# One decoder layer on one core: x1 kept in one layout, two normalisations moved from VectorE to ScalarE, other instruction orders

## The reference, cut to what matters

```
# 1. linear attention, 128 wide: q, k, v from x;
#    sq = elu(q)+1, sk = elu(k)+1
a  = (g*memory(sq, M, z) + (1-g)*causal(sq, sk, v)) @ w_o.T
x1 = layernorm(x + a)
# 2. convolution along the 512 columns; 8 positions make a head (32 heads)
kv[i,j] = ctx[i] * ctx[j]                 # i, j: positions of one head
y[i,j]  = conv(kv[i,j], kernel[head]) + D[head] * kv[i,j]
c[j]    = sum over i of y[i,j] * q[i]     # q is x1
x2 = layernorm(x1 + c)
# 3. gated feed-forward, 1408 wide, weights unpacked from 4 bits
h  = silu(x2 @ w_gate.T) * (x2 @ w_up.T)
x3 = layernorm(x2 + rmsnorm(h @ w_down.T))
```

## Time and profile before

| | |
|---|---|
| median of three runs | 532.0 us |
| the profiled execution | 532.28 us, its span 530.6 us |
| granted TensorE clock, mean | 0.988 |
| PE busy | 504.4 us (95%) |
| ACT busy | 400.5 us (75%) |
| POOL busy | 383.6 us (72%) |
| DVE busy | 370.9 us (70%) |
| DMA queue q1 | 98746 packets, 40.14 MB, 31.1% |
| packets under 512 B | 72570 |

### The profile page before, as it was taken

The page is one execution under the profiler, slowest core; times in us unless marked ns, Lnnn a source line. Parts: engine busy times, 40 slices in busy tenths (PEclk is TensorE's granted clock), DMA queues, the critical chain, the costliest instruction groups (busy, mean ns, idle before and its releaser), DMA issues.

```text
span 530.6 us, 11816 instructions
## 1 busy us (share of the span) xinstructions
PE 504.4 (95%) x3612; PEld 372.5 (70%) x3612; DVE 370.9 (70%) x1161; ACT 400.5 (75%) x962; POOL 383.6 (72%) x449
## 2 busy tenths in 40 slices
PE   8998986999999999999999999999999999999992
PEld 6776775668876677667766776777677667776651
DVE  2876665898887677867777787778686876674223
ACT  4478864046999988878877887888689868978981
POOL 2576883696899499959976996799679968972231
PEclk9999998999999999999999999999999999999997
DMA  8443766325026666313213320322041102001001
GB/s 230 138 100 82 167 142 134 79 56 140 12 61 132 156 111 150 71 48 115 56 24 86 86 62 4 114 64 59 0 119 40 40 1 80 2 2 40 1 21 40
DMA packets 98786, 40.63 MB, mean 77 GB/s; under 512 B 72570, under 2 KB 90106, under 8 KB 98746
## 3 DMA queue, kind: packets, MB, share of 16 engines
q1 hardware_dynamic: 98746, 40.14, 31.1%
HBM read 27.46 MB, written 12.66 MB: 76 GB/s over the span
## 4 chain that ended last, share of the span: by engine, by line
PE 67%; POOL 7%; issue 7%; SPq 6%; ACT 5%; DVE 3%; DMA 3%; POOLq 0%; DVEq 0%; ACTq 0%
PE p_cv L129 6%; PE p_cv L131 6%; PE p_cv L130 6%; PE p_n L1284 5%; PE p_n L1283 5%; PE p_n L1282 5%; SPq L401 5%; PE p_qk L1269 4%; PE p_x L1269 4%; PE p_x L1271 4%; PE p_qk L1271 4%; PE p_qk L882 3%; PE p_s L1269 3%; PE p_s L1271 3%; POOL shared L283 2%
## 5 line engine op out<-in xcount | busy, mean ns | idle before, releaser
L1120 ACT ACTIVATE p_qk<-p_qk,rescale 128x256 f32<-128x256 f32 x192 | 79.8, 464 | 24.6 <-PE p_qk L1271 24.2
L129 PE MATMUL p_cv<-kv_hi,toe 128*128 128x288 f16 x320 | 92.6, 289 | 5.9 <-DMA toe<-toeplitz_rows 4.5
L1088 POOL TENSOR_TENSOR h_lo<-w,h_hi 128x256 f16<-128x256 f32 x88 | 68.9, 795 | 35.6 <-ACT h_hi L1137 35.5
L130 PE MATMUL p_cv<-kv_lo,toe 128*128 128x288 f16 x320 | 92.5, 289 | 0.0
L131 PE MATMUL p_cv<-kv_hi,toe 128*128 128x288 f16 x320 | 92.5, 289 | 0.0
L283 POOL TENSOR_TENSOR shared<-shared 128x1024 f32<-128x1024 f32 x32 | 75.6, 2362 | 11.5 <-DVE shared L243 11.4
L1120 ACT ACTIVATE p_x<-p_x,rescale 128x256 f32<-128x256 f32 x192 | 79.8, 468 | 0.8
L1282 PE MATMUL p_n<-wd_hi,h_hi 128*128 128x512 f16 x176 | 66.7, 379 | 0.0
L1283 PE MATMUL p_n<-wd_lo,h_hi 128*128 128x512 f16 x176 | 66.7, 379 | 0.0
L1284 PE MATMUL p_n<-wd_hi,h_lo 128*128 128x512 f16 x176 | 66.7, 379 | 0.0
L1269 PE MATMUL p_qk<-x_hi,wg_hi 128*128 128x256 f16 x256 | 63.0, 273 | 2.4 <-DVE w L1183 1.5
(11 more groups left out here) (167 smaller groups left out, 1237.3 us busy)
## 6 DMA issues: line engine op xcount, KB each, us to landing
toe<-toeplitz_rows SPq DMA_DIRECT2D x16, 512.0 KB, 3.7
cnat<-in_ctx SPq DMA_DIRECT2D x128, 32.0 KB, 2.0
xq<-x_blocks SPq DMA_DIRECT2D x16, 256.0 KB, 5.6
xr<-x_rows SPq DMA_DIRECT2D x16, 256.0 KB
out_x<-fin SPq DMA_DIRECT2D x16, 256.0 KB
ring<-in_x SPq DMA_DIRECT2D x6, 512.0 KB, 4.1
...
```

The lines of the kernel that those rows point to most:

```text
L129: nc.tensor.matmul(dst, hi, kh, start=(mb == 0), stop=False)
L130: nc.tensor.matmul(dst, hi, kl, start=False, stop=False)
L1088: nc.gpsimd.tensor_tensor(h_lo[:, i, :], h32[:, i % 2, :], h_hi[:, i, :], ALU.subtract).then_inc(h_low, 1)
L1120: done = nc.scalar.activation(sums, sums, ACT.Copy, scale=rescale[:, p - 1, part * GI + i:part * GI + i + 1])
```

## The change

Parts of the change:

- `x1_blocks` is gone. A slot is stored by one DMA; its eight block stores go. q is loaded from `x1_rows` by `load_q`, 16 DMAs of 32 x 8 x 32 elements (32 KB) per group, where there were 2 of 256 KB. A semaphore `in_xq` counts to 128 per half.
- `xq` and `qv` are single tiles now. `turn_q` of a half waits for all 16 terms of the group before (8 before), and the first term of a group waits for both halves.
- x2's normalisation moves: VectorE forms `nm2 = -mean * rs` (128 x 1), ScalarE applies `x * rs + nm2` (`nx`). The same for x3: `e` is now VectorE's small `shift`, `z` is ScalarE's `finish`.
- In the first stage `means` and `variances` work on a slot's two columns one at a time (128 x 1 twice, not 128 x 2).
- All lists of order are new.

```
-        self.xq = [sb(f"xq{p}", [P, D], F32) for p in range(2)]
+        self.xq = sb("xq", [P, B, KD, 32], F32)
-        self.qv = [sb(f"qv{p}", [P, 2 * LB * 64], F32) for p in range(2)]
+        self.qv = sb("qv", [P, HG * 256], F32)
...
+    def norm_x2(g, t):
+        act.wait_ge(cv.nm2_made, g * 2 + t + 1)
+        nc.scalar.activation(cv.x2n[:, t, :], cv.x2n[:, t, :], ACT.Identity, scale=cv.rs2[:, t],
+                             bias=cv.nm2[:, t]).then_inc(cv.x2_made, 1)
...
     def turn_q(g, p):
-        dve.wait_ge(cv.in_xq[p], (g + 1) * 16)
-        wait(dve, cv.termed, (g - 1) * 16 + 8 * p + 8)
+        dve.wait_ge(cv.in_xq[p], (g + 1) * 128)
+        wait(dve, cv.termed, g * 16)
...
         if lb == 0:
-            dve.wait_ge(cv.q_kept, g * 2 + h // 2 + 1)
+            dve.wait_ge(cv.q_kept, g * 2 + 2)
...
-    def norm_x2(g, t):
+    def shift_x2(g, t):
         dve.wait_ge(cv.rs2_made, g * 2 + t + 1)
-        nc.vector.tensor_scalar(cv.x2n[:, t, :], cv.x2n[:, t, :], cv.mv2[:, t, 0:1], cv.rs2[:, t], ALU.subtract,
-                                ALU.mult).then_inc(cv.x2_made, 1)
+        nc.vector.scalar_tensor_tensor(out=cv.nm2[:, t], in0=cv.mv2[:, t, 0:1], scalar=-1.0, in1=cv.rs2[:, t],
+                                       op0=ALU.mult, op1=ALU.mult).then_inc(cv.nm2_made, 1)
...
         def store_x1(i):
             sp.wait_ge(x1_made, 2 * i + 2)
             sp.dma_start(tokens(x1_rows, i), ring[i % RING][:]).then_inc(x1_stored[i % RING], 16)
-            for e in range(2):
-                rows = ring[i % RING][:, e, :].rearrange("p (k f c) -> p k f c", f=4, c=32)
-                for f in range(4):
-                    block = x1_blocks[8 * (i // 4):8 * (i // 4) + 8, i % 4, 32 * f + 16 * e:32 * f + 16 * e + 16, :]
-                    sp.dma_start(block.rearrange("g s (k c) -> g s k c", c=32), rows[:, :, f, :]).then_inc(
-                        x1_blocked[i % RING], 16)
...
+        def load_q(g, k):
+            c = x1_rows[:, g * 32:g * 32 + 32, :].rearrange("b s (k f c) -> k f s b c", f=4, c=32)
+            for f in range(4):
+                sp.dma_start(cv.xq[32 * f:32 * f + 32, :, k, :], c[k, f]).then_inc(cv.in_xq[k // 2], 16)
...
         def means(i):
             dve.wait_ge(z_made, 2 * i + 2)
-            nc.vector.tensor_scalar(negmean[:, i, :], total[:, i, :], -1.0 / D, None, ALU.mult).then_inc(mean_made, 1)
+            for e in range(2):
+                done = nc.vector.tensor_scalar(negmean[:, i, e:e + 1], total[:, i, e:e + 1], -1.0 / D, None, ALU.mult)
+            done.then_inc(mean_made, 1)
...
+        def finish(f, t):
+            act.wait_ge(nm3_made[t], f + 1)
+            wait(act, stored[t], f * 16)
...
+            nc.scalar.activation(fin[:, t, :], z3[:, t, :], ACT.Identity, scale=rs3[:, t],
+                                 bias=nm3[:, t]).then_inc(fin_made[t], 1)
...
-        def finish(f, t):
+        def shift(f, t):
             dve.wait_ge(rs3_made[t], f + 1)
...
-            nc.vector.tensor_scalar(fin[:, t, :], z3[:, t, :], mv3[:, t, 0:1], rs3[:, t], ALU.subtract,
-                                    ALU.mult).then_inc(fin_made[t], 1)
+            nc.vector.scalar_tensor_tensor(out=nm3[:, t], in0=mv3[:, t, 0:1], scalar=-1.0, in1=rs3[:, t],
+                                           op0=ALU.mult, op1=ALU.mult).then_inc(nm3_made[t], 1)
...
-    ACT_ORDER = ("tl rs0_1 rs1_1 rs2_1 rs0_2 rs1_2 hk1 rs0_3 rs2_2 rs1_3 gu0 rs2_3 hh0 gu1 gu2 rs3_1 hh1 "
...
+    ACT_ORDER = ("rs0_1 hk1 rs1_1 rs2_1 rs0_2 rs1_2 rs2_2 rs0_3 rs1_3 rs2_3 tl gu0 gu1 hk2 hh0 hh1 gu2 rs3_1 "
```

More of the change, by code:

```diff
@@ L1009, in periods @@
     ss, ms, rr = (sb(n, [P, GT, 1], F32) for n in ("ss", "ms", "rr"))
[L1010 removed]
+    st3, mv3, ve3, rs3, nm3 = (sb(n, [P, GT, w], F32) for n, w in (
+        ("st3", 6), ("mv3", 2), ("ve3", 1), ("rs3", 1), ("nm3", 1)))
     warm = sb("warm", [P, 1], F32)
@@ L1052, in body @@
                     sp.wait_ge(cv.q_kept, it * 2 + p + 1)
-                    load_blocks(it + 1, p)
+                    for k in range(2 * p, 2 * p + 2):
+                        load_q(it + 1, k)
                 sp.wait_ge(cv.x2_summed, it * 2 - 2 + p + 1)
@@ L1248, in body @@
                     else:
-                        finish(n, t)
+                        shift(n, t)
         return body
@@ L1360, in decoder_layer @@
-    PE_ORDER = ("y1_0 g0_0 g1_0 g2_0 y1_1 y1_2 y1_3 y1_4 g0_1 g1_1 g2_1 y1_5 y1_6 g0_2 g1_2 c2 g0_3 g2_2 c3 "
[3 rows of a table removed]
-                "g10_3 y0_6 xt0 y0_7 y0_8 d0 y0_9 xt1 y0_10 d1").split()
-    DVE_ORDER = ("tm0 tm1 lk1 gu0 tm2 tm3 gu1 gu2 tm4 tm5 lk2 tm6 tm7 tm8 kt0 gu3 gu4 tm9 tm10 kt1 gu5 lk3 "
-                 "tm11 tm12 tm13 tm14 tm15 a1 kq0 kq1 gu6 gu7 bs0 b1 bn0 ln bs1 gu8 nm0 bn1 gu9 gu10 nm1 xt0 "
-                 "xt1 a0 b0 e0 e1").split()
-    ACT_ORDER = ("tl rs0_1 rs1_1 rs2_1 rs0_2 rs1_2 hk1 rs0_3 rs2_2 rs1_3 gu0 rs2_3 hh0 gu1 gu2 rs3_1 hh1 "
-                 "rs4_1 hk2 rs5_1 rs3_2 rs4_2 rs5_2 hh2 rs3_3 rs4_3 rs5_3 gu3 gu4 hh3 hh4 hk3 gu5 ho0 rs6_1 "
-                 "rs7_1 hh5 rs6_2 rs7_2 n1 rs8_1 rs6_3 rs8_2 rs7_3 gu6 gu7 kn rs8_3 hh6 rs9_1 rs10_1 ho1 "
-                 "rs9_2 rs10_2 gu8 rs9_3 rs10_3 hh7 hh8 gu9 gu10 hh9 xt0 hh10 xt1 n0").split()
@@ L1385, in decoder_layer @@
-    LAST_POOL = "hl0 hl1 hl2 hl3 a1 hl4 hl5 hl6 hl7 b1 hl8 hl9 hl10 A1 a0 B1 b0".split()
+    START_SYNC = ("x3 cx0 cx2 cx3 tw0 cx1 x4 st0 x5 cx6 toe0 st1 x6 st2 st3 xq2 xq0 xq1 xq3 toe1 cx7 xq4 xq6 "
+                  "cx4 xq5 x7 cx5 cx8 xq7 toe2 xr0 cx9 cx10 xr1 toe3 xr2 xq10 cx11 cx14 xq8 toe4 xq11 xr3 "
+                  "xq9 st4 st6 cx12 st5 st7 cx13 cx15 toe5").split()
+    START_PE = ("ze0 iw0 Xa0 Xb0 iw1 iw2 iw3 iz0 Q0 V0 Xa1 S0 M0 Xb1 w0 N0 Q1 T0 Oa0 w1 w2 Ob0 Xa2 S1 w3 V1 "
[9 rows of a table added]
+                "+y0_9 +y0_10 +xt1").split()
@@ new lines, in decoder_layer @@
+    PE_ORDER = ("y1_0 y1_1 y1_2 y1_3 y1_4 y1_5 y1_6 g0_0 g1_0 g2_0 c2 c3 g0_1 g1_1 g2_1 y1_7 g0_2 g1_2 c4 "
[3 rows of a table added]
+                "g10_3 xt0 y0_5 y0_6 y0_7 y0_8 y0_9 xt1 y0_10 d1").split()
+    DVE_ORDER = ("tm0 tm1 lk1 tm2 tm3 tm4 tm5 gu0 gu1 lk2 tm6 gu2 tm7 tm8 tm9 gu3 gu4 lk3 kt0 tm10 tm11 tm12 "
+                 "kt1 a1 gu5 tm13 gu6 gu7 tm14 tm15 b1 bs0 bn0 ln bs1 nm0 bn1 gu8 gu9 nm1 gu10 xt0 kq0 e1 a0 "
+                 "xt1 b0 e0 kq1").split()
+    ACT_ORDER = ("rs0_1 hk1 rs1_1 rs2_1 rs0_2 rs1_2 rs2_2 rs0_3 rs1_3 rs2_3 tl gu0 gu1 hk2 hh0 hh1 gu2 rs3_1 "
+                 "rs4_1 rs3_2 rs4_2 hh2 rs3_3 rs4_3 hk3 gu3 gu4 rs5_1 rs6_1 hh3 hh4 rs7_1 rs5_2 rs6_2 rs7_2 "
+                 "ho0 rs5_3 rs6_3 n1 gu5 gu6 rs7_3 hh5 rs8_1 hh6 gu7 hh7 rs9_1 rs10_1 kn rs8_2 rs9_2 rs10_2 "
+                 "ho1 rs8_3 rs9_3 rs10_3 nx0 gu8 gu9 xt0 hh8 gu10 hh9 nx1 hh10 xt1 n0 z1 z0").split()
@@ new lines, in decoder_layer @@
+    POOL_ORDER = ("pr1 pr2 tr0 hl0 hl1 pr3 hl2 tr1 hl3 tr2 hl4 a1 hl5 pn tr3 bn0 b1 hl6 hl7 bn1 hl8 hl9 hl10 "
+                  "a0 b0").split()
+    LAST_PE = ("y1_0 y1_1 y1_2 g0_0 g1_0 y1_3 y1_4 y1_5 g2_0 y1_6 y1_7 g0_1 g1_1 g2_1 y1_8 g0_2 g1_2 g2_2 "
[3 rows of a table added]
+               "w1_9 w1_10 y0_7 y0_8 y0_9 y0_10").split()
+    LAST_DVE = "gu0 gu1 a1 gu2 b1 gu3 gu4 e1 gu5 gu6 gu7 gu8 gu9 gu10 A1 B1 a0 b0 E1 e0".split()
+    LAST_ACT = ("rs0_1 rs1_1 rs2_1 rs0_2 rs1_2 rs2_2 rs0_3 tl rs1_3 gu0 rs2_3 hh0 gu1 n1 gu2 hh1 rs3_1 rs4_1 "
+                "rs5_1 rs3_2 rs4_2 rs5_2 hh2 rs3_3 rs4_3 rs5_3 gu3 gu4 hh3 gu5 rs6_1 rs7_1 rs6_2 hh4 rs7_2 "
+                "rs6_3 rs7_3 hh5 gu6 gu7 rs8_1 hh6 rs9_1 rs10_1 rs8_2 rs9_2 rs10_2 rs8_3 rs9_3 hh7 gu8 "
+                "rs10_3 hh8 gu9 gu10 hh9 hh10 ho0 z1 N1 ho1 n0 Z1 z0").split()
```

122 lines of the change are left out of this document (52 added, 70 removed), and 60 rows, old and new, of tables (LAST_PE, PE_ORDER, START_ACT, START_DVE).

## The result

The changed kernel takes 530.33 us (median of 20 runs, 529.92 to 530.95), the kernel before on the same chip 532.47 (529.33 to 535.53): ratio 0.9958, 95% interval 0.9944 to 0.9972. That is 2.1 us won, where 8.35 were forecast: clear of noise, and under the 0.5% from which the prediction speaks of faster. A second set of runs gave 530.25 against 532.2. The profiled execution spans 529.2 us, before 530.6; it was the longest of its 20 runs (530.95), so the traces show 1.4 us of the 2.1.

What follows compares the result with a forecast made beforehand. PE was taken to bound the rounds, so what it waits for in the first 91 us could be won. 7.1 + 1.6 - 1.5 + 1.5 - 0.35 = 8.35 us off some 532 gave 524.0 us, range 519.5 to 530.5.

Steps and rivals of the forecast that it cites:

- "same": Whole kernel: a time between 529.3 and 534.7 us, within the 0.5% bound; chance 0.12.
- One sign of being wrong: Named beforehand: rounds longer than 51.5 us, or a first term after 88 us.
- Start, +7.1: Start: waits for `toe0` and slot 6's load go, first term at 84.0 us instead of 91.06; 7.1 us won.
- clock, +1.6: Start of the convolution: without the 4.46 us idle PE stays at 2.4 GHz; 1.6 us won (0 to 2.2).
- ScalarE's stretch, -1.5: From 131.59 to 177.27 us: ScalarE has no room for its added x2 and slot 4 work; 1.5 us lost (0 to -3).
- Rounds, +1.5: Rounds: five PE waits of 0.3 us ahead of `g0_0` go, 1.5 us won.
- The margin of 0.3 us at `c2`: End of a round: `c2` comes at 6.5 us, its chain takes 6.2; nothing booked, -5 to 0 kept.
- the second rival: End of rounds: small shifts wait for GpSimd, up to 0.75 us on seven rounds, some 528.6 us; chance 0.12.
- The wait that goes: In five rounds PE's 0.3 us wait for VectorE's last product of h goes, as seven `y1` steps precede `g0_0`.
- Last lists, 0 booked: Last lists of order, near the span's end: the prediction has no term for their new order.
- End, -0.35: Last square to fin: VectorE's 0.55 us becomes a shift of 0.15 and ScalarE's 0.76; 0.35 us lost.
- The rival "slower": End of rounds: ScalarE's `z0` holds its queue until x3's statistics are finished; 536 us, chance 0.10.

Runs made afterwards that it cites:

- `toe0` alone: Kernel before with only the DMA `toe0` issued right behind `toe1`, ahead of slot 0's store: 530.03 us, ratio 0.994.
- the columns: Kernel before with only the slots' means and variances formed column by column: 531.76 us, ratio 0.9994.
- both: Kernel before with `toe0` moved ahead and means and variances column by column, block stores kept: 530.23 us, ratio 0.9967.
- either of two edits that share nothing else: Changed kernel with `nm2` and `nm3` formed by one-operand `tensor_scalar`: 524.51 us; or with only `kq1` moved to just behind `kq0`: 524.64 us.
- the fourth set of experiments: The one-operand kernel with the last lists of the kernel before (527.59 us), or with x3's finishing step on VectorE in the last lists alone (523.94 us).
- the one-operand kernel: Changed kernel with the shifts `nm2` and `nm3` formed by `tensor_scalar`, `rs` entering as a value for each partition: 524.51 us, ratio 0.9858.

## Why the prediction was wrong

The 530.33 lie 0.2 us inside the range of 519.5 to 530.5, at the end where the forecast of 524.0 has failed; "same" had a chance of 0.12. One sign of being wrong came: rounds longer than 51.5 us (51.54). Term by term, from PE's marks:

- *Start, +7.1, and clock, +1.6.* At the first feed-forward matmul 7.2 us are won (131.59 to 124.38), and the 1.5 us of `c3` are done as well: 8.7, as forecast. No wait for `toe0` or for a slot of x is left, the clock is 1.00 in every stretch above, the first term is at 84.80, forecast 84.0. "With no idle of 4 us PE stays at the 2.4 GHz level" was too loose a condition: waits of 3.2, 3.1 and 2.36 us in the experiments were followed by 0.50. The term held because no such wait is left. Its parts can't be added one by one, as the prediction did along one chain: `toe0` alone gives 4.0 at the convolution's first matmul (90.09 to 86.08), the columns 0.4, both 2.0, all of the change 5.9. Each of the two uncovers the loads behind the block stores; behind the columns' longer wait for slot 6 the clock is at 1.2 GHz for some 3 us.
- *ScalarE's stretch, -1.5.* Measured -0.5: the stretch to the first round lasts 43.39 us against 44.39, but with the 1.5 us of `c3` fewer in it. ScalarE is busy 42.31 of it, 97.5%. The prediction's own parts (1.5 and 1.5, less 1.3) give -1.7. Why the loss is smaller than either, no run shows. Together with the start 8.2, forecast 7.2.
- *Rounds, +1.5: the step that failed.* "So I book nothing, and keep -5 (0.7 in each of 7 rounds) to 0 for the margin." The margin of 0.3 us at `c2` was counted well: the shift lasts 1.09 us longer than the 0.15 booked and `c2` is held up by 0.82, so 0.27 were there. What was wrong is the 0.15. It is the second rival, to which the prediction gave 0.12, because "seldom so much, since the median was 0.3". The median is over eight places with and without a GpSimd instruction beside them; at the end of a round GpSimd starts `pr1` in the moment in which it has made the `rs` that the shift waits for, so the long case, 1221 ns in that row, comes every time. The rival's price, 0.75 us on seven rounds, was near the truth by two errors: a middle round loses 1.22 us, since the late product adds 0.33 to the 0.82 at `c2`, and there are six rounds. Undone, by either of two edits that share nothing else, it gives back 6.3 and 5.7 us between the first matmul of the convolution and the last matmul, 5.7 and 5.6 in the medians, and the kernel is then at 524.5, where 524.0 was forecast. With the shift short the five rounds give 1.85 (252.61 us for 254.46), booked 1.5.
- *The wait that goes.* The prediction put the 0.3 us of the earlier trace rows ahead of `g0_0`; the trace of before has it at `g9_0`, at 366.88, for a product of h. From start to start it is 0.46 us. It went all the same; `g9_0` has a new place, but no run tries it alone. The booked gain came and its reason was wrong: that is luck.
- *Last lists, 0 booked.* Measured -1.7, the short stops of the fourth set of experiments; the prediction didn't look at these lists, although they are new. It is the second term that failed, put at nothing without a reason. The last round adds -1.3: 0.8 for the shift (50.21 us for 49.41 without it) and 0.5 that no experiment split. That the one-operand kernel lands within 0.5 us of the forecast is therefore partly luck: 2.2 us that nobody booked stand against 1.0 more in ScalarE's stretch, 0.35 in the rounds and an execution that was 0.55 us early from the start.
- *End, -0.35.* From the last matmul to the end of the last normalisation it was 5.42 us and is 5.77, the -0.35 that were booked; the rest of the 0.6 lies in the last stores.

The rival "slower" had the right place, the end of the round, but the wrong engine: ScalarE finishes `z0` at 328.2 and goes straight to rescaling, and PE doesn't wait for it in the rounds.

The trace bears out the Trainium skill here. "SBUF — State Buffer", section "Who interferes with whom", says that an instruction of VectorE with both inputs in SBUF contends with GpSimd's reads, and that "Issue order, not op shape, decides who blocks": 1.24 us, 0.05 us behind `pr1`, is that; the same page lists `tensor_scalar` among those that can contend in a two-port mode, and on one column here it doesn't (0.17 to 0.22 us, 16 of 16). The prediction quoted the rule and then priced it by a median.
